# Scattering each slot's expert rows one slot later, and a reordered hand-over into the expert loop, in a GNN and mixture-of-experts kernel

## The chip, the cores and the metric

The kernel runs on one core of one Trainium2 chip. The metric is the device time of one execution in microseconds (us); lower is better. It is written at instruction level: each engine has its own program, and engines wait for one another by semaphores.

## The reference, cut to what matters

```python
# x 2048x512, adj 2048x2048
x = x + gnn(layernorm(x), adj)        # quantised: adj @ relu_q(x_q @ w_q), rounded to 4 bits
h = layernorm(x)
logits = h @ Wr + br                  # 16 experts
topk_w, topk_idx = top_k(softmax(logits), 2); topk_w /= sum(topk_w)
# per token and chosen expert e (hidden size 512):
t = gelu(layernorm(h @ W1[e] + b1[e]) * g1[e] + be1[e])
y = y + topk_w[e] * (t @ W2[e] + b2[e])
x = x + y
```

## The kernel before, in words

The first 200 us or so are the GNN: TensorE (PE) multiplies the adjacency, 128 rows at a time, with the rounded support. The result of each 128-row tile is stored to `out`, its normed copy to `xn_rows` in HBM, and the router's logits give each token two experts. Ranks and hit matrices are made into a table that lays the 4096 (token, expert) pairs out by expert in **slots** of 128 rows. One more piece of the first expert (the "early" slot, names with `e_`) is worked on before the table is complete. `dense` holds the gate values, which SP stores next to the normed rows in `xn_rows`; `tok_i` and `scat_i` are the token indices by slot, `plan` and `begins` packed words that say which expert each slot has and where an expert starts. `words_ps` is the product from which the plan is made, and `table_ok` says that it is there.

Then comes the expert loop, 38 slots, a pair in each trip, on four engines:

- **GpSimd (POOL)**, for slot number s, in this order: `slot_rstd(s + 1)`, the power that gives 1/sigma of the layer norm; `fetch(s)`, which waits for `gate_ok` of slot s + 3 and gathers the rows of slot s + 5 from `xn_rows` by an indirect DMA; `give`, which adds the finished rows of an earlier slot to `out` by an indirect DMA that accumulates. Scatters of neighbouring slots may overlap unless an expert starts between them, since one token is in two experts: `give` waits on `scattered` for that.
- **ScalarE (ACT)**: `slot_gelu(s)`, then `gated(s - 1)`, which turns the second layer's result in PSUM into gated rows `y_sb`, then `slot_x_hi(s + 3)` and `slot_gate(s + 3)` (the latter counts up `gate_ok`), then the rounding of the next expert's weights if one starts.
- **VectorE (DVE)**: `h_hat`, the low halves of the split operands and the statistics.
- **PE**: for slot s, `hidden_t(s)`, `layer_2(s - 1)`, `rows_t(s + 3)`, `layer_1(s + 2)`.

`y_sb` has two buffers, by the slot's parity. Every engine runs its own instructions in order. The lines below are not touched by the diff; they are what ties `gated` on ACT to the scatters on POOL (for slot s = 2j + par, so that `gated(n)` waits until the scatter of slot n - 2 has landed; each of the two semaphores starts at 16 from a store ahead of the loop):

```python
def gated(n, par, landed):
    act.wait_ge(mm2, n + 1)
    act.wait_ge(scattered[par], landed)
    act.activation(y_sb[:, par, :], y_ps(par), ACT.Copy, scale=gate[:, bass.ds(n + 1, 1)]).then_inc(y_ok, 1)
...
    gated(s - 1, 1 - par, landed)
    if not last:
        slot_x_hi(s + 3, 1 - par)
        slot_gate(s + 3, 1 - par, expert_in(word, par + 3))
...
    slot(j * 2 + par, par, word, j * 16 + 16 * par)
```

Of the kernel before, what the change touches and what calls it, by code (L numbers as in the profile page):

```python
# [27 lines left out]
I32 = mybir.dt.int32  # L28
AX_X = mybir.AxisListType.X

P = 128
N = 2048
D = 512
E = 16
T = N // P
C = D // P
# [149 lines left out]
def gnn_moe_program(nc, x, adj_steps, gnn_w, scalars, wr, br, w1, b1, g1, be1, w2, b2, consts, xn_rows, bias_dram, out):  # L186
    with ExitStack() as ctx:
# [5 lines left out]
        def place(name, shape, dt):  # L193
            size = int(np.prod(shape[1:])) * 4
            t = nc.alloc_sbuf_tensor_at(name, shape, dt, offset=where[0])
            where[0] += (size + 31) // 32 * 32
            assert where[0] <= usable, (name, where[0], usable)
            return t

        def sem(name):  # L200
            return ctx.enter_context(nc.semaphore(name))
# [4 lines left out]
        g1_sb = place("g1_sb", [P, E * C], F32)  # L206
        be1_sb = place("be1_sb", [P, E * C], F32)
# [15 lines left out]
        scat_i = place("scat_i", [P, TAB], I32)  # L223
# [55 lines left out]

        e_xg = place("e_xg", [P, ROW], F32)  # L280
        e_h_hat = e_xg[:, 0:D]
        e_y = e_xg[:, 0:D]
        e_gate = place("e_gate", [P, 1], F32)
        e_small = place("e_small", [P, 16], F32)
        e_tok = place("e_tok", [P, 4], I32)
        where[0] = end_gnn - D * 4
        e_g = place("e_g", [P, D], F32)
        where[0] = xg_at
        xg = place("xg", [P, 2, ROW], F32)
        xg1 = place("xg1", [P, ROW], F32)  # L290
# [11 lines left out]
        gt_hi = place("gt_hi", [P, 2, D], F32R)  # L302
        gt_lo = place("gt_lo", [P, 2, D], F32R)
        y_sb = place("y_sb", [P, 2, D], F32)
        idx_s = place("idx_s", [P, 3], I32)
        h_stats = place("h_stats", [P, 2, 6], F32)
        h_mv = place("h_mv", [P, 2, 2], F32)
        h_rs = place("h_rs", [P, 2, 4], F32)
# [26 lines left out]
        def const(name):  # L335
            a, b = COLS[name]
            return k_sb[:, a:b]
# [5 lines left out]
        small_in = sem("small_in")  # L343
# [44 lines left out]
        picked = sem("picked")  # L388
# [23 lines left out]
        idx_ok = sem("idx_ok")  # L412
# [72 lines left out]
        def load_begins(eng, j):  # L485
            return eng.value_load(begins[0:1, bass.ds(j, 1)], min_val=0, max_val=3)

        def expert_in(word, i):

            return (word >> (FIELD * i)) & (E - 1)  # L490
# [116 lines left out]
        @block.gpsimd  # L607
        def _(pool):
            own = Chain(pool, pool_own)
            for h in range(2):  # L610
                half = slice(h * E * C // 2, (h + 1) * E * C // 2)
                pool.dma_start(g1_sb[:, half], g1[:, half]).then_inc(small_in, 16)
                pool.dma_start(be1_sb[:, half], be1[:, half]).then_inc(small_in, 16)
            pool.dma_start(br_sb[:, :], br).then_inc(small_in, 16)
            pool.dma_start(wr_sb[:, :], wr).then_inc(small_in, 16)
            neg_half = const("neg_half")
# [47 lines left out]
            def dense_gates(b):  # L664

                t0, n = GATED[b]
                tiles = slice(t0, t0 + n)
                first, second = (gates[:, 2 + k, tiles].unsqueeze(2).to_broadcast([P, n, E]) for k in range(2))
                if b < 3:
                    pool.wait_ge(gate_parts, b + 1)  # L670
                pool.tensor_tensor(scratch[:, tiles, :], mask[:, 1, tiles, :], second, ALU.mult)
                own.link(pool.tensor_tensor(dense[:, tiles, :], mask[:, 0, tiles, :], first, ALU.mult))
                pool.tensor_tensor(dense[:, tiles, :], dense[:, tiles, :], scratch[:, tiles, :], ALU.add).then_inc(dense_ok, 1)

            def last_gates():

                t0, n = GATED[3]
                tiles = slice(t0, t0 + n)
                pool.wait_ge(picked, 5)
                pool.wait_ge(exp_ok, 5)  # L680
                own.link(pool.tensor_scalar(gates[:, 2, tiles], gates[:, 1, tiles], 1.0, None, ALU.add))
                own.link(pool.tensor_tensor(gates[:, 2, tiles], gates[:, 2, tiles], const("minus_one").to_broadcast([P, n]), ALU.pow))
                own.link(pool.tensor_tensor(gates[:, 3, tiles], gates[:, 1, tiles], gates[:, 2, tiles], ALU.mult))

            def row_hits(b, first, last):

                pool.wait_ge(placed_ok, b + 1)
                if not b:
                    pool.wait_ge(split_lo[0], 1)
                if b in (1, 2):  # L690
                    pool.wait_ge(table_mm, b)
                if b >= 3:
                    pool.wait_ge(adj_mm, STEPS + WINDOWS + 1)
                for j in range(first, last):
                    ins = pool.tensor_scalar(hit_sets[HIT_SET[b]][1][:, j, :], const("minus_row"),
                                             where_f[:, b % 2, 0, j % 2, j // 2:j // 2 + 1], None, ALU.is_equal)
                if last == (2 if b == 4 else 2 * BATCHES[b][1]):
                    ins.then_inc(rows_hit, 1)
# [36 lines left out]
            early_rstd()  # L735
            row_hits(3, 4, 6)
            last_gates()
            row_hits(4, 0, 2)
            dense_gates(3)

            def gather(s):
                to, landed = (xg1[:, :], first_in) if s == 1 else (xg[:, s % 2, :], gathered)
# [8 lines left out]
            def slot_rstd(s, par):  # L751

                pool.wait_ge(h_var, s + 1)
                pool.tensor_tensor(h_rs[:, par, 0:1], h_rs[:, par, 2:3], neg_half, ALU.pow).then_inc(h_rstd, 1)
# [6 lines left out]
            rest = pool.value_load(pairs[0:1, 0:1], min_val=E // 2 - 2, max_val=SLOTS // 2 - 2)  # L761
# [6 lines left out]
            def add_rows(at, par):  # L768
                pool.sem_inc(pool_turn, 1)
                pool.indirect_dma_start(  # L770
                    out, bass.IndirectOffsetOnAxis(ap=at, axis=0),
                    y_sb[:, par, :], None, compute_op=ALU.add).then_inc(scattered[par], 16)

            def give(s, start):

                pool.wait_ge(scattered[s % 2], s // 2 * 16 + 16)
                pool.wait_ge(scattered[1 - s % 2], start * 16 + (s + 1) // 2 * 16)
                pool.wait_ge(y_ok, s + 3)
                add_rows(scat_i[:, s:s + 1], s % 2)
# [6 lines left out]
            slot_rstd(2, 0)  # L786
            fetch(1)
            pool.wait_ge(e_scattered, 16)
            give(0, 1)
            def pool_pair(j):  # L790
                earlier, word = load_begins(pool, j - 1), load_begins(pool, j)
                for s in (2 * j, 2 * j + 1):
                    slot_rstd(s + 1, (s + 1) % 2)
                    fetch(s)
                    give(s - 1, (word & 1) if s % 2 else (earlier >> 1))

            for j in range(1, SURE + 1):
                pool_pair(j)
# [6 lines left out]
            def give_last(back, done, starts):  # L805

                par = (3 - back) % 2
                pool.wait_ge(scattered[par], done)
                pool.wait_ge(scattered[1 - par], starts)
                pool.wait_ge(y_ok, rest * 2 + (4 + back))  # L810
                add_rows(idx_s[:, back:back + 1], par)

            pool.tensor_copy(idx_s[:, :], scat_i[:, bass.ds(rest * 2 + 1, 3)]).then_inc(idx_ok, 1)
            earlier, word = load_begins(pool, rest), load_begins(pool, rest + 1)
            slot_rstd(rest * 2 + 3, 1)
            pool.wait_ge(idx_ok, 1)
            give_last(0, rest * 16 + 16, (earlier >> 1) * 16 + rest * 16 + 16)
            give_last(1, rest * 16 + 32, (word & 1) * 16 + rest * 16 + 16)
            give_last(2, rest * 16 + 32, (word >> 1) * 16 + rest * 16 + 32)
# [7 lines left out]
        def _(act):  # L827
# [143 lines left out]
            store_xn(T - 2)  # L971
            gate_exp(3)
            finish_t(T - 2)
            act.wait_ge(small_in, 96)
            act.wait_ge(last_xn_ok, 1)
            store_xn(T - 1)
            finish_t(T - 1)
# [28 lines left out]
            word = load_plan(act, 0)  # L1006
            rest = act.value_load(pairs[0:1, 0:1], min_val=E // 2 - 2, max_val=SLOTS // 2 - 2)
# [46 lines left out]
            word = load_plan(act, rest + 1)  # L1054
# [457 lines left out]
        def _(pe):  # L1512
# [230 lines left out]
            def first_layer_1_end():  # L1743

                pe.wait_ge(x_lo_ok, 1)
                first_part(xt_lo, 0, last=True).then_inc(mm1, 1)

            pe.wait_ge(tables_in, 16)
            pe.wait_ge(rounded, 1)
            pe.wait_ge(small_in, 96)  # L1750
            for hs in range(2 * WINDOWS):
                half_step(hs)
                for t in range(T - 2):
# [34 lines left out]
            for h in range(2):  # L1788
                ins = pe.matmul(compact_ps, tab_sb[:, h, :], sel[:, h, :].bitcast(F32), start=h == 0, stop=h == 1)
            ins.then_inc(compact_mm, 1)  # L1790
            for kind in range(3):
                for h in range(2):
                    col = 2 * kind + h
                    ins = pe.matmul(words_ps[:, kind * TAB:(kind + 1) * TAB], word_r[:, col:col + 1].to_broadcast([P, P]),
                                    sel[:, h, :], start=h == 0, stop=h == 1)
            ins.then_inc(words_mm, 1)
            first_layer_1_end()
            early_layer_2_lo()
            early_layer_2_end()

# [40 lines left out]
            word = load_plan(pe, 0)  # L1841
            rest = pe.value_load(pairs[0:1, 0:1], min_val=E // 2 - 2, max_val=SLOTS // 2 - 2)
# [24 lines left out]
            before, word = expert_in(load_plan(pe, rest), 1), load_plan(pe, rest + 1)  # L1867
# [57 lines left out]
```

## Time and profile before

| | |
|---|---|
| median of 3 runs | 503.92 us (502.75 to 504.37) |
| the profiled execution | 503.04 us, its span 501.3 us |
| mean granted TensorE clock | 0.984 |
| busy in the span | PE 461.6 us (92%), DVE 348.6 (70%), ACT 285.7 (57%), POOL 233.8 (47%) |
| instructions | 10204 |

The span is what the profiler recorded, 1.7 us less than the execution's own time. In the rows further down, a timeline row is start, duration, engine, source line, operation, output<-inputs; what stands in brackets is how long the engine had been idle before it, and who released it. An indirect DMA's row is the time in which POOL makes its descriptors, and not the transfer, which goes on after it.

### The profile page before, as it was taken

The page shows a single profiled execution, that of the slowest core. Times are in us where ns is not written, and L with a number is a line of the kernel's source. Part 1 is how long each engine was busy: PE and PEld are TensorE (multiplying, and loading weights), DVE is VectorE, ACT ScalarE, POOL GpSimd, SP SyncE. Part 2 cuts the span into 40 slices and gives each one's busy share as a digit, 9 for nine tenths or more (in the row PEclk, how much of TensorE's full clock was granted, in tenths as well). Part 3 has the DMA queues.
Part 4 walks back from the last instruction along what each step waited for, and adds up shares of the span by engine and source line. Part 5 has one row for each costly group of instructions (what it writes and reads, how often), then busy time and mean ns, then how long its engine had stood idle before and what let it go on. Part 6 is the DMA issues. An engine that isn't in the chain of part 4 may idle for free. (4 is left out here: it accounts for less than half of the span.)

```text
span 501.3 us, 10204 instructions
## 1 busy us (share of the span) xinstructions
PE 461.6 (92%) x2297; PEld 379.3 (76%) x2298; DVE 348.6 (70%) x735; ACT 285.7 (57%) x472; POOL 233.8 (47%) x271
## 2 busy tenths in 40 slices
PE   0789999999999999989989999999999999999970
PEld 0568888887888888867868888887888778888850
DVE  5898873868778867875487677486878767786410
ACT  1667453564443442545747857668778865776440
POOL 5364320431174635742464546554455444556531
PEclk9999999999999999989999999999999999999995
DMA  8621224984546362349676876956888888464433
GB/s 288 273 84 43 85 74 165 329 304 149 189 150 228 132 194 103 127 110 310 202 160 162 248 211 140 229 148 165 248 256 230 253 285 195 96 149 73 83 50 42
DMA packets 31451, 87.26 MB, mean 174 GB/s; under 512 B 6016, under 2 KB 6224, under 8 KB 30912
## 3 DMA queue, kind: packets, MB, share of 16 engines
q1 hardware_dynamic: 17488, 56.54, 34.2%
q0 software_dynamic: 9328, 22.02, 21.4%
q10 hardware_dynamic: 4608, 8.39, 4.5%
q8 instruction: 11, 0.18, 0.1%
q14 instruction: 16, 0.13, 0.1%
HBM read 67.79 MB, written 19.14 MB: 173 GB/s over the span
## 5 line engine op out<-in xcount | busy, mean ns | idle before, releaser
L743 POOL DMA_INDIRECT xg<-xn_rows,tok_i x40 | 48.7, 1218 | 86.7 <-ACT gate L967 76.9
L1015 ACT ACTIVATE g_sb<-ps,be_sb,g_sb 128x128 f32<-128x128 f32 x152 | 57.2, 457 | 49.0 <-PE ps L1829 49.0
L770 POOL DMA_INDIRECT out<-y_sb,scat_i x35 | 61.4, 1755 | 28.4 <-DMA out<-y_sb,scat_i 14.6
L1442 DVE TENSOR_TENSOR w_split<-w_raw,w_split x56 | 66.0, 1221 | 9.9 <-issue 9.7
L1450 DVE TENSOR_SCALAR h_hat<-ps,h_mv,h_rs 128x512 f32<-128x512 f32 x38 | 30.7, 809 | 47.1 <-issue 28.4
L833 ACT ACTIVATE adj_hi<-adj_raw,small 128x1024 fp32r<-128x1024 f32 x32 | 36.8, 1150 | 40.6 <-PE ps L1564 34.6
L1001 ACT ACTIVATE w_split<-w_raw x28 | 53.0, 1914 | 4.5 <-DMA w_raw<-in_w 2.6
L1132 DVE SCALAR_TENSOR_TENSOR adj_lo<-adj_raw,small,adj_hi 128x1024 fp32r<-128x1024 f32 x32 | 40.8, 1275 | 19.7 <-ACT adj_hi L833 19.6
L1564 PE MATMUL ps<-sup,adj_lo 128*128 128x512 f32 x192 | 49.2, 398 | 0.0
L1564 PE MATMUL ps<-sup,adj_hi 128*128 128x512 f32 x192 | 49.2, 398 | 0.0
L654 POOL TENSOR_SCALAR rstd<-mv 128x1 f32<-128x1 f32 x15 | 13.7, 915 | 66.7 <-DVE mv L1172 66.7
L1807 PE MATMUL ps<-w_split,gt_hi 128*128 x152 | 41.3, 393 | 0.0
L1810 PE MATMUL ps<-w_split,gt_lo 128*128 x152 | 41.1, 392 | 0.0
L1813 PE MATMUL ps<-w_split,gt_hi 128*128 x152 | 40.8, 390 | 0.0
L994 ACT ACTIVATE y_sb<-ps,gate 128x512 f32<-128x512 f32 x38 | 26.1, 686 | 25.6 <-PE ps L1813 23.8
L1564 PEld LDWEIGHTS ps<-sup,adj_lo 128*128 128x128 f32 x192 | 34.9, 188 | 6.9
L1564 PEld LDWEIGHTS ps<-sup,adj_hi 128*128 128x128 f32 x192 | 35.0, 188 | 6.8
L1807 PE MATMUL ps<-w_split,xt_hi 128*128 x148 | 40.0, 392 | 0.0
L1810 PE MATMUL ps<-w_split,xt_lo 128*128 x148 | 39.8, 390 | 0.0
L1813 PE MATMUL ps<-w_split,xt_hi 128*128 x148 | 39.7, 390 | 0.0
L1668 PE MATMUL ps<-bias_row,two_rows 128*128 (+1 forms) x78 | 37.2, 477 | 0.3 <-DVE x_sb L1166 0.3
L1375 DVE BATCH_NORM_STATS2 h_stats<-ps 128x6 f32<-128x512 f32 x38 | 26.3, 693 | 12.3 <-PE ps L1813 7.5
(212 smaller groups left out, 954.8 us busy)
## 6 DMA issues: line engine op xcount, KB each, us to landing
w_raw<-in_w SPq DMA_DIRECT2D x64, 512.0 KB
adj_raw<-in_adj_steps SPq DMA_DIRECT2D x32, 512.0 KB, 3.5
out<-x_sb ACTq DMA_DIRECT2D x16, 256.0 KB, 2.9
xn_rows<-xn ACTq DMA_DIRECT2D x16, 256.0 KB, 2.7
x_sb<-in_x SPq DMA_DIRECT2D x3, 1024.0 KB, 12.7
gw_raw<-in_gnn_w SPq DMA_DIRECT2D x1, 1024.0 KB, 5.0
x_sb<-in_x SPq DMA_DIRECT2D x2, 512.0 KB, 6.6
xg<-xn_rows,tok_i POOLq DMA_INDIRECT x40, 3.4
```

Of the source, the lines that this page charges most:

```text
L743: return pool.indirect_dma_start(to, None, xn_rows, bass.IndirectOffsetOnAxis(ap=tok_i[:, s:s + 1], axis=0)).then_inc(landed[s % 2], 16)
L770: pool.indirect_dma_start(out, bass.IndirectOffsetOnAxis(ap=at, axis=0), y_sb[:, par, :], None, compute_op=ALU.add).then_inc(scattered[par ...
L833: act.activation(adj_hi[:, par, :], adj_raw[:, par, :], ACT.Copy, scale=small[:, 0:1]).then_inc(adj_hi_ok, 1)
L1001: act.activation(w_parts(n, 0, e + 1), w_raw[:, n, :, :].rearrange("p a n -> p (a n)")[:, at], ACT.Copy).then_inc(split_hi[n], 1)
L1015: ins = act.activation(g_sb[:, par, c * P:(c + 1) * P], ht_ps(par)[:, c * P:(c + 1) * P], ACT.Gelu, scale=g1_sb[:, bass.ds(e * C + c, 1)], ...
L1132: dve.scalar_tensor_tensor(adj_lo[:, par, :], adj_raw[:, par, :], small[:, 0:1], adj_hi[:, par, :].bitcast(F32), ALU.mult, ALU.subtract).t ...
L1442: ins = dve.tensor_tensor(w_parts(n, 1, e + 1, 2 * h, 2), w_raw[:, n, :, :].rearrange("p a n -> p (a n)")[:, at], w_parts(n, 0, e + 1, 2 * ...
L1564: ins = pe.matmul(acc_bank(t), part[:, n % 2, k * P:(k + 1) * P], sup[:, first_k + k, :], start=first_k + k == 0 and not half, stop=first_ ...
L1668: pe.matmul(dst, two_rows[:, :], bias_row[n][:, row], start=True, stop=False)
L1807: pe.matmul(dst, act_hi[:, par, c * P:(c + 1) * P], w_part(n, 0, e, c), start=False, stop=False)
L1810: pe.matmul(dst, act_lo[:, par, c * P:(c + 1) * P], w_part(n, 0, e, c), start=False, stop=False)
L1813: ins = pe.matmul(dst, act_hi[:, par, c * P:(c + 1) * P], w_part(n, 1, e, c), start=False, stop=c == C - 1)
```

## The change

- In the expert loop POOL scatters the rows of slot s - 2 where it scattered those of slot s - 1. The scatter ahead of the loop is gone, and four are behind it instead of three (`give_last(-1, ...)` is new, `idx_s` has four columns). `y_sb`, its two buffers and the wait in `gated` stay.
- Ahead of the loop, PE does the last four products of slot 0's first layer (`first_layer_1_end`) before the six small ones from which the plan is made.
- `last_gates` on POOL no longer waits for `picked`; that wait stands in front of `dense_gates(3)`, which now comes ahead of `row_hits(4, 0, 2)`.
- `g1` and `be1` are loaded by one DMA each, not two, so that POOL issues two fewer at the start.
- The early slot's result `e_y` has the place of `e_g` and not of `e_xg`.

```diff
@@ -279,12 +279,12 @@
         e_h_hat = e_xg[:, 0:D]
-        e_y = e_xg[:, 0:D]
...
         e_g = place("e_g", [P, D], F32)
+        e_y = e_g[:, :]
@@ -302,7 +302,7 @@
-        idx_s = place("idx_s", [P, 3], I32)
+        idx_s = place("idx_s", [P, 4], I32)
@@ -607,10 +607,8 @@
-            for h in range(2):
-                half = slice(h * E * C // 2, (h + 1) * E * C // 2)
-                pool.dma_start(g1_sb[:, half], g1[:, half]).then_inc(small_in, 16)
-                pool.dma_start(be1_sb[:, half], be1[:, half]).then_inc(small_in, 16)
+            pool.dma_start(g1_sb[:, :], g1).then_inc(small_in, 16)
+            pool.dma_start(be1_sb[:, :], be1).then_inc(small_in, 16)
@@ -676,7 +674,6 @@
                 tiles = slice(t0, t0 + n)
-                pool.wait_ge(picked, 5)
                 pool.wait_ge(exp_ok, 5)
@@ -735,8 +732,9 @@
             last_gates()
+            pool.wait_ge(picked, 5)
+            dense_gates(3)
             row_hits(4, 0, 2)
-            dense_gates(3)
@@ -786,13 +784,12 @@
             pool.wait_ge(e_scattered, 16)
-            give(0, 1)
             def pool_pair(j):
-                earlier, word = load_begins(pool, j - 1), load_begins(pool, j)
+                earlier = load_begins(pool, j - 1)
                 for s in (2 * j, 2 * j + 1):
                     slot_rstd(s + 1, (s + 1) % 2)
                     fetch(s)
-                    give(s - 1, (word & 1) if s % 2 else (earlier >> 1))
+                    give(s - 2, 1 if s == 2 else (earlier >> 1) if s % 2 else (earlier & 1))
@@ -808,12 +805,13 @@
-                add_rows(idx_s[:, back:back + 1], par)
-
-            pool.tensor_copy(idx_s[:, :], scat_i[:, bass.ds(rest * 2 + 1, 3)]).then_inc(idx_ok, 1)
+                add_rows(idx_s[:, back + 1:back + 2], par)
+
+            pool.tensor_copy(idx_s[:, :], scat_i[:, bass.ds(rest * 2, 4)]).then_inc(idx_ok, 1)
...
+            give_last(-1, rest * 16 + 16, (earlier & 1) * 16 + rest * 16)
             give_last(0, rest * 16 + 16, (earlier >> 1) * 16 + rest * 16 + 16)
@@ -1788,13 +1786,13 @@
             ins.then_inc(compact_mm, 1)
+            first_layer_1_end()
             for kind in range(3):
...
             ins.then_inc(words_mm, 1)
-            first_layer_1_end()
             early_layer_2_lo()
```

How the change moves instructions, at three places. First POOL where the loop is entered, before the change: `h_rs` is `slot_rstd`, `xg<-xn_rows` a gather, `out<-y_sb` a scatter, and a row of L777 is the ordering wait in `give`.

```order
L754 TENSOR_TENSOR h_rs<-h_rs,k_sb 128x1 [waits h_var]
L743 DMA xg<-xn_rows,tok_i 128x528 [waits gate_ok]
L770 DMA out<-y_sb,scat_i 2176x512 [waits y_ok,scattered1,e_scattered,scattered0]
L486 TENSOR_LOAD begins
L486 ISA x2
L486 TENSOR_LOAD begins
L486 ISA x2
L754 TENSOR_TENSOR h_rs<-h_rs,k_sb 128x1 [waits h_var]
L743 DMA xg<-xn_rows,tok_i 128x528 [waits gate_ok]
L777 ISA [waits scattered1]
L770 DMA out<-y_sb,scat_i 2176x512 [waits scattered0,y_ok]
```

The same place with the change (lines stand two lower):

```order
L752 TENSOR_TENSOR h_rs<-h_rs,k_sb 128x1 [waits h_var]
L741 DMA xg<-xn_rows,tok_i 128x528 [waits gate_ok]
L486 TENSOR_LOAD begins [waits e_scattered]
L486 ISA x2
L752 TENSOR_TENSOR h_rs<-h_rs,k_sb 128x1 [waits h_var]
L741 DMA xg<-xn_rows,tok_i 128x528 [waits gate_ok]
L768 DMA out<-y_sb,scat_i 2176x512 [waits y_ok,scattered0,scattered1]
L752 TENSOR_TENSOR h_rs<-h_rs,k_sb 128x1 [waits h_var]
L741 DMA xg<-xn_rows,tok_i 128x528 [waits gate_ok]
```

The first scatter, that of slot 0, moved behind the next `h_rs` and the next gather, and each later one with it.

Second, POOL ahead of the loop, before the change: `gates` is `last_gates`, `scratch` and `dense` are `dense_gates(3)`, and `hit_row_139` is `row_hits(4, 0, 2)`.

```order
L681 TENSOR_SCALAR gates<-gates 128x5 [waits exp_ok,picked]
L682 TENSOR_TENSOR gates<-gates,k_sb 128x5 [waits pool_own]
L683 TENSOR_TENSOR gates<-gates 128x5 [waits pool_own]
L695 TENSOR_SCALAR hit_row_139<-k_sb,where_f 128x128 [waits adj_mm,placed_ok,pool_own]
L695 TENSOR_SCALAR hit_row_139<-k_sb,where_f 128x128
L671 TENSOR_TENSOR scratch<-mask,gates 128x80
L672 TENSOR_TENSOR dense<-mask,gates 128x80
L673 TENSOR_TENSOR dense<-dense,scratch 128x80 [waits pool_own]
```

And with the change:

```order
L678 TENSOR_SCALAR gates<-gates 128x5 [waits exp_ok]
L679 TENSOR_TENSOR gates<-gates,k_sb 128x5 [waits pool_own]
L680 TENSOR_TENSOR gates<-gates 128x5 [waits pool_own]
L669 TENSOR_TENSOR scratch<-mask,gates 128x80 [waits picked,pool_own]
L670 TENSOR_TENSOR dense<-mask,gates 128x80
L671 TENSOR_TENSOR dense<-dense,scratch 128x80 [waits pool_own]
L692 TENSOR_SCALAR hit_row_139<-k_sb,where_f 128x128 [waits adj_mm,placed_ok]
L692 TENSOR_SCALAR hit_row_139<-k_sb,where_f 128x128
```

The wait for `picked` went from the first row to the fourth, and the three `dense_gates` rows ahead of the two hit rows.

Third, PE just ahead of the loop, before the change: `sel,tab_sb` is the table product, `sel,word_r` the products for the plan, and `w_split,xt_lo` is `first_layer_1_end`.

```order
L1789 MATMUL ps<-sel,tab_sb 128x54 [waits xn_t_ok,sel_ok,tab_ok]
L1789 MATMUL ps<-sel,tab_sb 128x54
L1794 MATMUL ps<-sel,word_r 128x54 x6
L1727 MATMUL ps<-w_split,xt_lo 128x512 [waits x_lo_ok]
L1727 MATMUL ps<-w_split,xt_lo 128x512 x3
L1673 MATMUL ps<-w_split,bias_hi 128x512 [waits split2_lo]
```

And with the change:

```order
L1787 MATMUL ps<-sel,tab_sb 128x54 [waits xn_t_ok,sel_ok,tab_ok]
L1787 MATMUL ps<-sel,tab_sb 128x54
L1725 MATMUL ps<-w_split,xt_lo 128x512 [waits x_lo_ok]
L1725 MATMUL ps<-w_split,xt_lo 128x512 x3
L1793 MATMUL ps<-sel,word_r 128x54 x6
L1671 MATMUL ps<-w_split,bias_hi 128x512 [waits split2_lo]
```

The four products of slot 0's layer one went ahead of the six for the plan.

## Rows read from the trace of the kernel before

**Rows 1.** The page's first part: busy us, share of the span, instructions.

```profile
PE 461.6 (92%) x2297; PEld 379.3 (76%) x2298; DVE 348.6 (70%) x735; ACT 285.7 (57%) x472; POOL 233.8 (47%) x271
```

**Rows 2.** Stages: length, busy us (instructions) by engine, granted clock, DMA share, GB/s.

```profile
300.00:340.00 40.00, 40.00 (x200) 33.06 (x199) 26.42 (x43) 26.96 (x51) 22.73 (x18) 1.00 0.72 181
...
216.00:218.00 2.00, 2.00 (x6) 1.62 (x5) 0.97 (x2) 0.04 (x1) 1.10 (x1) 0.50 0.00 0
```

**Rows 3.** Timeline late in the loop, ACT and POOL, slots 33 to 35.

```profile
465.29 0.69 ACT L994 ACTIVATE y_sb<-ps,gate 128x512 f32<-128x512 f32 x1 [0.78 <-PE ps L1813]
...
466.84 1.36 POOL L743 DMA_INDIRECT xg<-xn_rows,tok_i  x1 [2.31 <-DMA out<-y_sb,scat_i]
...
468.51 1.61 POOL L770 DMA_INDIRECT out<-y_sb,scat_i  x1 [0.30 <-issue]
...
472.12 0.69 ACT L994 ACTIVATE y_sb<-ps,gate 128x512 f32<-128x512 f32 x1 [0.74 <-PE ps L1813]
...
475.00 1.59 POOL L770 DMA_INDIRECT out<-y_sb,scat_i  x1 [0.30 <-issue]
...
479.26 0.69 ACT L994 ACTIVATE y_sb<-ps,gate 128x512 f32<-128x512 f32 x1 [1.11 <-PE ps L1813]
```

**Rows 4.** Timeline where the loop is entered, ACT, POOL and PE.

```profile
239.49 1.64 POOL L770 DMA_INDIRECT out<-y_sb,scat_i  x1 [0.30 <-issue]
...
241.54 0.69 ACT L994 ACTIVATE y_sb<-ps,gate 128x512 f32<-128x512 f32 x1 [0.88 <-PE ps L1813]
...
248.67 0.69 ACT L994 ACTIVATE y_sb<-ps,gate 128x512 f32<-128x512 f32 x1 [1.04 <-DMA out<-y_sb,scat_i]
...
252.51 0.66 PE L1829 MATMUL ps<-k_sb,h_hat 128*128 128x128 f32 x4 [0.96 <-DVE h_hat L1450]
...
260.91 0.66 PE L1829 MATMUL ps<-k_sb,h_hat 128*128 128x128 f32 x4 [1.27 <-DVE h_hat L1450]
```

**Rows 5.** Timeline of POOL, two neighbouring scatters, the second waiting.

```profile
400.35 2.04 POOL L770 DMA_INDIRECT out<-y_sb,scat_i  x1 [1.53 <-DMA out<-y_sb,scat_i]
...
410.44 1.58 POOL L770 DMA_INDIRECT out<-y_sb,scat_i  x1 [4.79 <-DMA out<-y_sb,scat_i]
```

**Rows 6.** DMA busy tenths, 466 to 494 us in 40 slices of 0.7 us.

```profile
DMA  6000559795000365978000009881000058996860
```

**Rows 7.** Timeline of POOL behind the loop, the scatters of slots 35 and 36.

```profile
480.80 1.62 POOL L770 DMA_INDIRECT out<-y_sb,idx_s  x1 [3.47 <-ACT y_sb L994]
486.87 1.56 POOL L770 DMA_INDIRECT out<-y_sb,idx_s  x1 [4.44 <-issue]
```

**Rows 8.** DMA queues, 241 to 441 us: packets, MB, share of 16 engines.

```profile
q1 hardware_dynamic: 7017, 25.30, 39.0%
```

**Rows 9.** Timeline ahead of the loop, POOL, PE and DVE.

```profile
208.99 0.34 POOL L681 TENSOR_SCALAR gates<-gates 128x5 f32<-128x5 f32 x1 [1.76 <-DVE so_far L1226]
...
214.15 0.68 DVE L1371 TENSOR_TENSOR xt_lo<-ps,xt_hi 128x512 fp32r<-128x512 f32 x1
...
214.78 0.83 PE L1794 MATMUL ps<-sel,word_r 128*128 128x54 f32 x6
...
215.44 2.03 PE L1727 MATMUL ps<-w_split,xt_lo 128*128 128x512 f32 x4
...
216.41 1.10 POOL L743 DMA_INDIRECT xg<-xn_rows,tok_i  x1 [2.77 <-DMA xn_rows<-dense]
...
217.51 0.70 DVE L1375 BATCH_NORM_STATS2 h_stats<-ps 128x6 f32<-128x512 f32 x1 [1.03 <-PE ps L1727]
...
218.64 0.32 DVE L1424 TENSOR_SCALAR fields<-ps 128x162 f32<-128x162 f32 x1
...
219.86 0.42 PEld L1721 LDWEIGHTS ps<-k_sb,xg 128*128 128x128 f32 x4 [0.26 <-DMA xg<-xn_rows,tok_i]
```

**Rows 10.** Timeline of the first microseconds, POOL.

```profile
3.22 0.53 POOL L613 DMA_DIRECT2D be_sb<-in_be  x1
...
10.31 0.60 POOL L626 TENSOR_TENSOR x_pow<-x_pow,k_sb 128x1 f32<-128x1 f32 x1 [3.66 <-DVE x_pow L1094]
```

More of the change, by code:

```diff
@@ L973, in _ @@
             finish_t(T - 2)
-            act.wait_ge(small_in, 96)
+            act.wait_ge(small_in, 64)
             act.wait_ge(last_xn_ok, 1)
@@ L1749, in _ @@
             pe.wait_ge(rounded, 1)
-            pe.wait_ge(small_in, 96)
+            pe.wait_ge(small_in, 64)
             for hs in range(2 * WINDOWS):
```

## The prediction, made before the changed kernel ran

> **What bounds the kernel now.** I read the page's first part first: PE is busy for 92% of the span and POOL for 47% [rows 1]. The table of stages then says where PE is the limit: 40.00 of 40 us between 300 and 340, with 200 matmuls, at the full granted clock [rows 2]. So in the expert loop nobody holds PE up, except at its entry, where two gaps stand in its timeline (0.96 and 1.27 us, both for `h_hat`) [rows 4]. One slot takes 6.83 us there (from one `y_sb` write to the next) [rows 3], and over the loop 6.99 us: `y_sb` of slot 1 is written at 241.54 [rows 4], that of slot 35 at 479.26 [rows 3], 34 slots in 237.72 us.
>
> Next I read who waits for a scatter, since that is what moves. The wait of ACT on `scattered` bites once before the change: `y_sb` of slot 2 at 248.67, released by the DMA of slot 0's scatter, which POOL had issued at 239.49 [rows 4]. In all other slots the scatter lies so far back that the wait is met, and that distance is what the change uses up.
>
> **The scatter one slot later: the term that decides.** `gated(n)` on ACT may write its buffer only when the scatter of slot n - 2 has landed, and this stays. The late rows give the distances. ACT writes `y_sb` at 465.29, and when it has copied the gate, POOL gathers at 466.84 and scatters at 468.51; the next `y_sb` is written at 472.12 [rows 3]. The scatter at 468.51 is that of the slot just written, and the write that needs its buffer is the next but one, at 479.26: the distance is 479.26 - 468.51 = 10.75 us. With the change, the scatter at this place is that of the slot before, whose buffer is wanted at 472.12, so 472.12 - 468.51 = 3.61 us are left.
>
> How long does a scatter take? From the start of its row to the end of its transfer, where the DMA engines are otherwise quiet: the one issued at 480.80 [rows 7] has its data moving from slice 24 to slice 27 of the DMA row, so until about 485.6 [rows 6], 4.8 us; that of 468.51 [rows 3] ends in slice 9, by 473.0 [rows 6], 4.5 us at most. POOL's next ordered scatter started 6.07 us after 480.80 [rows 7], so a released engine starts some time after the data. With ACT I put 0.6 us on top of 4.6: 5.2 us in the quiet case (an estimate; its lower end is 4.5 with nothing on top). Where weights are loaded too, it is longer: 248.67 - 239.49 = 9.18 us on ACT [rows 4], 410.44 - 400.35 = 10.09 us on POOL [rows 5]. All of it is above 3.61 us.
>
> So ACT will stand still in every slot, and that is a ring, since ACT's own instructions release the scatter: `gated(n - 1)` → gate copy → `gate_ok` → POOL's gather → scatter of n - 2 → it lands → `gated(n)`. Its length is the new time of a slot. The first half is 468.51 - 465.29 = 3.22 us, or 475.00 - 472.12 = 2.88 [rows 3]; I take 3.1. The second half is the scatter's: 5.2 in quiet, some 8.0 beside loads (the two rows less 1 to 2 us, since they are ones long enough to be seen waiting). The loads' queue held 39% of the DMA engines' time from 241 to 441 us, with the other queue beside it [rows 8]. The same bytes spread over a longer loop meet fewer of the scatters, so I take 45% of slots as loaded: 0.45 x 8.0 + 0.55 x 5.2 = 6.5 us. The ring is then 3.1 + 6.5 = 9.6 us, against 6.99 now. From `gated(1)`, the last that needs no scatter, to `gated(35)` that is 34 x (9.6 - 6.99) = **+88.7 us**. The bounds: all quiet, 34 x (2.88 + 5.2 - 6.99) = +37 us; all loaded, 34 x (3.22 + 8.0 - 6.99) = +144 us. Nothing is hidden below the lower one, unless a scatter comes back in under 3.9 us (6.99 - 3.1), which no row shows.
>
> A rule of the skill speaks on just this number. The Trainium skill (DMA: Bandwidth & Descriptors, section on the anatomy of one DMA on the SWDGE path) fits a DMA from GpSimd as 2.0 us plus its bytes at 436 GB/s, 2.6 us for the 256 KB here; by it the ring would be 5.7 us and hold nobody. The DMA row disagrees: 4.5 to 4.8 us in the quietest stretch.
>
> What else stands in the ring's shadow: PE will wait 9.6 - 6.83 = 2.8 us in a slot, for `xt_hi` that ACT writes behind `gated`. DVE's split of it and the statistics come later with it. POOL's `slot_rstd` runs once in each round, behind the scatter, and PE uses its result a slot later.
>
> **The four behind the loop.** In place of three; the scatter of slot 34 needs nothing but its turn. Those of 35, 36 and 37 follow their `y_sb` as before, and `gated(36)` and `gated(37)` follow the landings of 34 and 35: 480.80 is 1.54 us behind 479.26, and 486.87 is 7.61 behind it [rows 3, 7], distances that already hold one landing. One more scatter on the queue: 0 to 2 us, I take 0.5.
>
> **The hand-over.** The layer's four products (2.03 us, in a stretch where the granted clock is 0.50 [rows 2]) go ahead of the six small ones (0.83 us) [rows 9]. PE begins the six at 214.78, and `xt_lo`, for which the four wait, is there at 214.15 + 0.68 = 214.83, so that they can begin at about 214.9 and end at 217.0 instead of 217.47; the statistics start at about 217.0 instead of 217.51 [rows 9], the power and `h_hat` with them, and the plan's DVE work behind them too: -0.5 us. The six small ones end at about 217.8, before DVE wants them at 218.1, half a microsecond ahead of the 218.64 of before [rows 9]. The gates: without `picked` POOL's row at 208.99, idle for 1.76 us before it, can begin at about 207.6 [rows 9], and `dense` is done some 2.8 us sooner; the gather at 216.41 waited for that store, and will next wait for `tok_i`, which DVE makes from the table product; I take it as 1.0 us sooner. PE had idled 0.26 us for it [rows 9], so it adds at most that. I take -0.5 us for the whole, bounds 0 and -1. If the cover of the small products is gone (DVE waiting for the plan), it costs their 0.83 us.
>
> **Things at nothing.** Two DMA issues fewer at the start save 2 x 0.53 us of POOL, which then idles 3.66 us for DVE anyhow [rows 10]. The place of `e_y` and the fourth index column change no work. The two gaps of 0.96 and 1.27 us at the entry [rows 4] would go, since POOL no longer stands in front of a scatter there; but the ring is longer than the slot with its gap, so this gives nothing more: they are in the 6.99.
>
> **Sum.** 88.7 + 0.5 - 0.5 = +88.7 us on the profiled 503.04, which lies 0.9 below the median of the three runs: 503.9 + 88.7 = 592.6; I say 591, as both estimated shares lean high.
>
> **The rivals.**
> - *No ring, and faster* (3%). If scatters came back within 3.61 us (the point from which it decides), ACT would never wait, and POOL would do the next slot's `slot_rstd` without standing behind a landing. Then the two gaps go: 503.9 - 0.96 - 1.27 - 0.5 = 501.2. For it: only the page's 2.6 us. Against it: every landing that a row shows. No change, within 0.3% (502.4 to 505.4): 2%.
> - *A ring in loaded slots only* (4%). If the quiet landing fits into the slot after all, say because the gather goes out sooner against the scatter, only some 15 slots pay about 2 us: +30, or 534.
> - *PE's clock becomes the bound* (4%). PE now pauses in each slot. The granted clock did fall to 0.50, at 216 to 218, after a stretch of small products and waits [rows 2, 9]. If it stayed at that level (1.2 GHz for 2.4) through the loop, a slot would be twice 6.83, 13.7 us: 34 x 6.7 = +227, or 731. Against it: layer two of slot n needs only what `gated(n - 2)` released, and after it has two rounds (19.2 us) for one and a half slots of work; at half speed PE would also be busy without a pause. The Trainium skill (TensorE: Matmul & The Clock Gate, Part 1) has the clock halved after idling and doubled after sustained work, by which it would toggle and hide under the ring.
>
> **How the numbers follow.** The ring in every slot has 87%, at 591, between 541 and 647. The range 552 to 628 leaves 7% of that at its ends and the 13% of the others outside, so it holds 80%. Faster by over 0.3% (what a measurement of this kernel can tell) 3%, within it 2%, slower 95%.
>
> **What would show it.** In the profile of the changed kernel: `y_sb` on ACT idle in nearly every slot, released by the DMA of `out<-y_sb`, 3 to 4 us each; a scatter 3.1 us behind each `y_sb`; the loop's `y_sb` rows 8.1 to 11 us apart, farther while weights are loaded and nearest 8.1 at the end; PE's share down from 92% to about 78%; `h_stats` of slot 0 half a microsecond sooner. It is wrong if the `y_sb` rows stay near 6.9 us apart, or if the wait in a slot is for PE.

## The result: 13.7% slower, 572.02 us

| | before | with the change |
|---|---|---|
| median | 503.34 us (502.59 to 504.37, 4 runs) | 572.02 us (570.62 to 574.83, 4 runs) |
| ratio | | 1.1372, 95% interval 1.1344 to 1.1401 |
| span of the profiled run | 501.3 us | 573.1 us |
| mean granted TensorE clock | 0.984 | 0.971 |

The forecast was 591, with a range of 552 to 628. The cause that it named is in the profile; the size was 19 us too large. The profiled execution of the changed kernel took 574.83 us, 2.8 above the median, so its rows add up to a little more than the medians differ.

The page of the changed kernel first: busy time, share of the span and instructions by engine, then three of its costliest groups, with the idle time in front of them and who ended it.

```profile
PE 478.5 (84%) x2297; PEld 383.9 (67%) x2298; DVE 350.9 (61%) x735; ACT 284.3 (50%) x472; POOL 227.0 (40%) x269
...
L741 POOL DMA_INDIRECT xg<-xn_rows,tok_i x40 | 44.6, 1116 | 192.6 <-ACT gate L965 188.4
L992 ACT ACTIVATE y_sb<-ps,gate 128x512 f32<-128x512 f32 x38 | 26.2, 688 | 135.3 <-DMA out<-y_sb,scat_i 131.6
L1440 DVE TENSOR_TENSOR w_split<-w_raw,w_split x56 | 66.1, 1221 | 10.5 <-ACT w_split L999 7.3
```

PE's work is the same 2297 matmuls, but 84% and not 92% of the span [rows 1]. `y_sb` on ACT, which sat idle for a scatter's DMA once before (1.04 us) [rows 4], does so for 131.6 us. The list of waits says how often (engine and line that waited, for whom, us in all, times, longest):

```profile
POOL xg L741 <- ACT gate L965: 188.4, 37, 8.9
ACT y_sb L992 <- DMA out<-y_sb,scat_i: 131.6, 34, 8.9
DVE xt_lo L1369 <- ACT xt_hi L960: 72.7, 27, 6.5
...
PE ps L1827 <- DVE h_hat L1448: 37.1, 24, 2.6
```

34 times, which is every slot but the first two, which need no scatter, and the two written behind the loop, which wait for the scatters of `idx_s`. The table of stages has the 40 us that stood in [rows 2]: PE did 153 matmuls in it, not 200, and was busy for 33.31 us and not 40.00. The DMA engines had less to do, too (0.62 for 0.72).

```profile
300.00:340.00 40.00, 33.31 (x153) 26.04 (x152) 21.51 (x35) 22.03 (x43) 16.22 (x15) 0.96 0.62 165
```

The ring itself, late in the loop where no weights are loaded; first ACT and then POOL in the changed kernel's timeline (start, duration, engine, line, operation; in brackets the idle time and its releaser):

```profile
527.43 0.69 ACT L992 ACTIVATE y_sb<-ps,gate 128x512 f32<-128x512 f32 x1 [2.54 <-DMA out<-y_sb,scat_i]
...
528.50 0.20 ACT L965 ACTIVATE gate<-xg  x1
...
535.21 0.69 ACT L992 ACTIVATE y_sb<-ps,gate 128x512 f32<-128x512 f32 x1 [3.30 <-DMA out<-y_sb,scat_i]
...
543.10 0.69 ACT L992 ACTIVATE y_sb<-ps,gate 128x512 f32<-128x512 f32 x1 [4.38 <-DMA out<-y_sb,scat_i]
...
528.99 1.02 POOL L741 DMA_INDIRECT xg<-xn_rows,tok_i  x1 [4.34 <-ACT gate L965]
530.31 1.56 POOL L768 DMA_INDIRECT out<-y_sb,scat_i  x1 [0.30 <-issue]
531.37 1.12 POOL L752 TENSOR_TENSOR h_rs<-h_rs,k_sb 128x1 f32<-128x1 f32 x1
536.76 1.02 POOL L741 DMA_INDIRECT xg<-xn_rows,tok_i  x1 [4.27 <-ACT gate L965]
538.09 1.59 POOL L768 DMA_INDIRECT out<-y_sb,scat_i  x1 [0.31 <-issue]
```

Read it as a circle: `y_sb` at 527.43, gate copy, gather at 528.99, scatter at 530.31 (2.88 us behind `y_sb`), and the next `y_sb` at 535.21, 4.90 us behind the scatter. 2.88 + 4.90 = 7.78 us, and the slot takes just that. The same circle with a weight load beside it:

```profile
377.88 0.69 ACT L992 ACTIVATE y_sb<-ps,gate 128x512 f32<-128x512 f32 x1 [0.85 <-DMA out<-y_sb,scat_i]
378.95 0.20 ACT L965 ACTIVATE gate<-xg  x1
379.44 1.73 POOL L741 DMA_INDIRECT xg<-xn_rows,tok_i  x1 [3.91 <-ACT gate L965]
...
380.88 0.82 SPq L532 DMA_DIRECT2D w_raw<-in_w  x2
381.47 1.57 POOL L768 DMA_INDIRECT out<-y_sb,scat_i  x1 [0.30 <-issue]
...
382.75 0.87 SPq L532 DMA_DIRECT2D w_raw<-in_w  x2
390.09 0.69 ACT L992 ACTIVATE y_sb<-ps,gate 128x512 f32<-128x512 f32 x1 [7.08 <-DMA out<-y_sb,scat_i]
```

SP issues the loads of two layers around the scatter, each in two halves; the scatter comes back after 8.62 us, and the slot takes 12.21 us. POOL's gather took 1.73 us here and not 1.02, so the first half of the circle was longer too (3.59 us). Over the whole loop, `y_sb` of slot 1 is written at 244.60 and that of slot 35 at 551.31:

```profile
244.60 0.69 ACT L992 ACTIVATE y_sb<-ps,gate 128x512 f32<-128x512 f32 x1 [0.89 <-PE ps L1811]
...
551.31 0.69 ACT L992 ACTIVATE y_sb<-ps,gate 128x512 f32<-128x512 f32 x1 [2.75 <-DMA out<-y_sb,scat_i]
```

306.71 us for 34 slots, 9.02 us each, against 6.99. By the distances between the `y_sb` rows, 11 of these slots took 9.4 to 12.6 us (11.36 on average, their scatters back after 8.3 us), and 23 took 7.6 to 8.5 (7.90 on average, their scatters back after 5.0). In each of the 11, SP issued a weight load between 1.5 us before and 0.9 us after the start of the scatter's row. Of the 23, one had a load issued while its scatter was out, 3.6 us behind the row's start. The span grew by 71.8 us: 69.0 in these 34 slots, 3.1 ahead of them (slot 1 at 244.60 and not 241.54; see the first experiment), and -0.3 behind them.

### The profile page after: what moved, and what is told of

The parts are those of the page before. It is cut to its first block and busy times, and to the rows that moved or that the text cites. A ratio compares the mean times of both kernels' runs of the same rounds, so it can differ in the third digit from the quotient of the medians.

```text
span 573.1 us, 10152 instructions
## 1 busy us (share of the span) xinstructions
PE 478.5 (84%) x2297; PEld 383.9 (67%) x2298; DVE 350.9 (61%) x735; ACT 284.3 (50%) x472; POOL 227.0 (40%) x269
## 5 line engine op out<-in xcount | busy, mean ns | idle before, releaser
L741 POOL DMA_INDIRECT xg<-xn_rows,tok_i x40 | 44.6, 1116 | 192.6 <-ACT gate L965 188.4
L992 ACT ACTIVATE y_sb<-ps,gate 128x512 f32<-128x512 f32 x38 | 26.2, 688 | 135.3 <-DMA out<-y_sb,scat_i 131.6
L1369 DVE TENSOR_TENSOR xt_lo<-ps,xt_hi 128x512 fp32r<-128x512 f32 x39 | 26.9, 690 | 72.7 <-ACT xt_hi L960 72.7
L768 POOL DMA_INDIRECT out<-y_sb,scat_i x34 | 53.8, 1581 | 10.4 <-issue 10.4
L1827 PE MATMUL ps<-k_sb,h_hat 128*128 128x128 f32 x152 | 24.6, 285 | 39.5 <-DVE h_hat L1448 37.1
L1130 DVE SCALAR_TENSOR_TENSOR adj_lo<-adj_raw,small,adj_hi 128x1024 fp32r<-128x1024 f32 x32 | 40.8, 1276 | 19.7 <-ACT adj_hi L831 19.6
L1827 PEld LDWEIGHTS ps<-k_sb,h_hat 128*128 128x128 f32 x152 | 16.7, 141 | 52.7 <-DVE h_hat L1448 48.5
L1805 PE MATMUL ps<-w_split,xt_hi 128*128 x148 | 42.5, 411 | 9.4 <-ACT xt_hi L960 9.4
L752 POOL TENSOR_TENSOR h_rs<-h_rs,k_sb 128x1 f32<-128x1 f32 x38 | 44.1, 1160 | 4.4 <-DVE h_rs L1376 4.3
L1808 PE MATMUL ps<-w_split,gt_lo 128*128 x152 | 43.8, 413 | 0.0
L1805 PE MATMUL ps<-w_split,gt_hi 128*128 x152 | 43.7, 411 | 0.0
L1811 PE MATMUL ps<-w_split,gt_hi 128*128 x152 | 42.3, 401 | 0.3 <-DVE w_split L1440 0.2
L1811 PE MATMUL ps<-w_split,xt_hi 128*128 x148 | 39.8, 390 | 0.5 <-DVE w_split L1440 0.5
```

The lines of the kernel that those rows point to most:

```text
L741: return pool.indirect_dma_start(to, None, xn_rows, bass.IndirectOffsetOnAxis(ap=tok_i[:, s:s + 1], axis=0)).then_inc(landed[s % 2], 16)
L768: pool.indirect_dma_start(out, bass.IndirectOffsetOnAxis(ap=at, axis=0), y_sb[:, par, :], None, compute_op=ALU.add).then_inc(scattered[par ...
L1130: dve.scalar_tensor_tensor(adj_lo[:, par, :], adj_raw[:, par, :], small[:, 0:1], adj_hi[:, par, :].bitcast(F32), ALU.mult, ALU.subtract).t ...
L1805: pe.matmul(dst, act_hi[:, par, c * P:(c + 1) * P], w_part(n, 0, e, c), start=False, stop=False)
L1808: pe.matmul(dst, act_lo[:, par, c * P:(c + 1) * P], w_part(n, 0, e, c), start=False, stop=False)
L1811: ins = pe.matmul(dst, act_hi[:, par, c * P:(c + 1) * P], w_part(n, 1, e, c), start=False, stop=c == C - 1)
```

## The experiments

Nine runs were made, one kernel among them twice, on three occasions, each beside the kernel before on the same chip; the ratio is what counts. Two theories: the **ring** (`gated` waits for the scatter of two slots back, and that scatter now follows the `y_sb` just ahead), and its rivals (POOL's new order or a late scatter costs by itself; the hand-over has a part in it).

| kernel | median us | before there | ratio, 95% interval |
|---|---|---|---|
| hand_over_only | 502.72 | 502.20 | 1.0005 (0.9982 to 1.0028) |
| scatter_only | 571.76 | 502.20 | 1.1356 (1.1297 to 1.1415) |
| scatter_before_gate | 500.15 | 502.20 | 0.9963 (0.9938 to 0.9987) |
| scatter_then_gather | 553.01 | 502.20 | 1.1018 (1.0965 to 1.1071) |
| four_buffers | 505.94 | 503.02 | 1.0056 (1.0032 to 1.0079) |
| thin_loads | 535.73 | 503.02 | 1.0645 (1.0611 to 1.0679) |
| scatter_before_gate_2 | 501.79 | 503.38 | 0.9971 (0.9951 to 0.9992) |
| before_gate_no_hand_over | 502.37 | 503.38 | 0.9989 (0.9974 to 1.0004) |
| before_gate_four_buffers | 499.97 | 503.38 | 0.9946 (0.9920 to 0.9971) |

### The two halves of the change

`hand_over_only` is the kernel before with the diff's parts on `g1`/`be1`, `e_y`, `last_gates`, `dense_gates(3)` and `first_layer_1_end`; `scatter_only` has the other parts (`idx_s`, `give(s - 2, ...)`, `give_last(-1, ...)`).

> The kernel before with all of the change except the scatter: sooner gates, slot 0's layer one ahead of the words, two DMA issues fewer, e_y on e_g. The statistics of slot 0 started 1.03 us sooner in the changed kernel, so my sum now allows 0 to -1.0 us, middle -0.5: 502.9. Rival: a part of the 69 us comes from the hand-over, since slot 1's y_sb was written at 244.60 there and at 241.54 before; by it this kernel is slower by up to 3 us, 506.

> The kernel before with the later scatter alone. If the ring through ACT's wait for the landed scatter is the whole cause, 571 to 573, within 1.5 us of the changed kernel. If the hand-over costs 3 us of its own, 569 or less.

The scatter alone is 571.76, as the ring theory expected: all of the loss. The hand-over alone makes no difference that this measurement can tell. The rows of `hand_over_only` that answer to [rows 9], and the table product just ahead of them (`sel,tab_sb`):

```profile
214.28 0.62 PE L1787 MATMUL ps<-sel,tab_sb 128*128 128x54 f32 x4 [0.56 <-ACT tab_sb L985]
...
216.34 0.69 DVE L1373 BATCH_NORM_STATS2 h_stats<-ps 128x6 f32<-128x512 f32 x1
...
219.84 0.66 PE L1719 MATMUL ps<-k_sb,xg 128*128 128x128 f32 x4 [1.29 <-DMA xg<-xn_rows,tok_i]
...
221.37 1.11 PE L1827 MATMUL ps<-k_sb,h_hat 128*128 128x128 f32 x4 [0.88 <-issue]
235.52 0.66 PE L1719 MATMUL ps<-k_sb,xg 128*128 128x128 f32 x4 [1.77 <-DMA xg<-xn_rows,tok_i]
```

The statistics start at 216.34 (217.51 before), yet PE's next product with gathered rows is where it was (219.84, with 1.29 us of idle time for the gather in front of it). Most of that 1.17 us is not the new order's doing. The kernel before had the table product at this time:

```profile
214.34 0.62 PE L1789 MATMUL ps<-sel,tab_sb 128*128 128x54 f32 x4 [0.52 <-ACT tab_sb L987]
```

Counted from the table product, all eleven traces compare:

| traces | granted clock where the four products ran | statistics behind the table product | gathered product behind it |
|---|---|---|---|
| before | 0.50 | 3.17 us | 5.54 us |
| two others with the old order (`scatter_only`, `before_gate_no_hand_over`) | 1.00 | 2.32 us | 5.50 and 5.63 us |
| the eight with the new order | 1.00 | 2.06 to 2.07 us | 5.41 to 5.56 us |

So at the same clock the new order brings the statistics 0.25 us sooner, and PE's next product, which waits for the gather, not at all. A further 0.85 us is the clock, which was low there in the trace of before and in no other.

The 3.1 us at the loop's entry are not shown to be the hand-over's either. Slot 1's `y_sb` stood between 240.5 and 244.6 us in the kernels with the hand-over; without it, it stood at 244.07 in `scatter_only` and at 241.33 in `before_gate_no_hand_over`. What goes with a late entry is the clock. In four traces it fell to 0.50 for 2 to 4 us around 224 (0.91 on average from 220 to 240), and there slot 1's `y_sb` came 28.4 to 30.2 us behind the table product. In the other seven it stayed at 1.00 from 220 to 240, and that distance was 26.1 to 27.2 us. `scatter_only`, with the old order, is one of the four. PE had waited alike ahead of it in both kinds (1.2 to 1.5 us for the gather, then 0.9), so what decides is open. PE's wait for a later gather, near 235 us, differs too: 3.06 us in the changed kernel, the longest, 1.77 in `hand_over_only` and 1.45 in `scatter_only`.

### Cutting the ring at POOL

```diff
                 for s in (2 * j, 2 * j + 1):
                     slot_rstd(s + 1, (s + 1) % 2)
-                    fetch(s)
                     give(s - 2, 1 if s == 2 else (earlier >> 1) if s % 2 else (earlier & 1))
+                    fetch(s)
```

> The changed kernel with the scatter of slot s-2 behind slot_rstd(s+1) as changed, but ahead of the wait for the gate instead of behind the gather. That cuts one edge of the ring: the scatter no longer follows the y_sb before it. Ring theory: 6.9 us a slot again, 501 to 504 us in all, with the two gaps at the loop's entry (0.96 and 1.27 us) gone. Rival (a scatter that is late by one slot costs by itself, by its order behind the power or by its meeting the loads): 540 or more.

500.15 us, a little under the expected 501 to 504, and 6.99 us a slot in its profile: the ring no longer sets the time, with the same scatter (slot s - 2), the same `slot_rstd` ahead of it and the same four behind the loop. What decided was that the scatter stood behind the wait for a gate which ACT copies after the `y_sb` before. ACT still waited for a scatter 11 times, 29.2 us in all and up to 5.0 at a time, but those waits hardly reached PE, which waited 3.7 us from 236 to 490 us (3.9 before).

### Cutting it at ACT

`y_sb` gets seven buffers where the adjacency was: four used in turn in the loop, three for the last slots. The wait in `gated` is for one scatter of the same parity less.

```diff
+                to = y_sb[:, at, :] if at is not None else y_sb[:, n & 3, :] if isinstance(n, int) else \
+                    y_sb[:, :, :].rearrange("p a d -> p (a d)")[:, bass.ds((n & 3) * D, D)]
-                act.wait_ge(scattered[par], landed)
+                if at is None and not (isinstance(landed, int) and landed <= 16):
+                    act.wait_ge(scattered[par], landed - 16)
...
-            with act.Fori(1, SURE + 1) as j:
+            act_pair(1)
+            with act.Fori(2, SURE + 1) as j:
...
-                    y_sb[:, par, :], None, compute_op=ALU.add).then_inc(scattered[par], 16)
+                    y_sb[:, slot, :], None, compute_op=ALU.add).then_inc(scattered[par], 16)
```

> The changed kernel with its POOL order untouched, but four y_sb buffers in the loop instead of two (three more for the slots behind it), so that ACT waits for the scatter of slot n-4 and not n-2. That cuts the ring at its other edge. Ring theory: 6.9 us a slot, 501 to 504 us. Rival (POOL's order, or contention of late scatters, and not the buffer): 560 or more.

505.94 us, with POOL's order untouched. So neither the order nor the lateness costs 69 us; the buffer's wait does. It is 2 us above the range that I had expected, and 0.56% above the kernel before: the four buffers with this order leave a cost of their own. POOL's list of waits from 236 to 490 us (line, for whom, us in all, times, longest) is where one looks:

```profile
POOL xg L743 <- ACT gate L972: 52.4, 28, 3.4
POOL out L770 <- DMA out<-y_sb,scat_i: 27.6, 9, 4.6
POOL h_rs L754 <- DVE h_rs L1387: 16.8, 15, 3.9
```

POOL stands before a scatter for the landing of another 9 times, 27.6 us in all; in the kernel before it was 6 times and 14.6 us over the same stretch. These are the ordering waits where an expert starts, with the next slot's power and gather queued behind them. That this is the 3 us is not shown: over the same stretch PE's own waits add up to 4.9 us, against 3.9 in the kernel before. `before_gate_four_buffers`, below, has the same buffers and is faster than before, so the buffers by themselves don't cost it.

### Making the ring shorter

```diff
                     slot_rstd(s + 1, (s + 1) % 2)
-                    fetch(s)
+                    pool.wait_ge(gate_ok, s + 4)
                     give(s - 2, 1 if s == 2 else (earlier >> 1) if s % 2 else (earlier & 1))
+                    gather(s + 5)
```

> The changed kernel with scatter and gather exchanged behind the wait for the gate: the ring is shorter by the gather's 1.02 us and the 0.30 us behind it, 1.33 us. Quiet slots go from 7.84 to the 6.85 that PE needs (22 of them, -22 us), loaded ones from some 11.3 to 10.0 (12, -16 us): 534 us, between 526 and 540. If something else than this ring sets the slot's time, the exchange changes little: 565 or more.

553.01 us, so 19 us gone and not 38; the expectation was missed. The way it was worked out is what failed, as the timeline shows (ACT's `y_sb` and gate, then POOL):

```profile
505.11 0.69 ACT L993 ACTIVATE y_sb<-ps,gate 128x512 f32<-128x512 f32 x1 [1.76 <-DMA out<-y_sb,scat_i]
506.17 0.20 ACT L966 ACTIVATE gate<-xg  x1
512.53 0.69 ACT L993 ACTIVATE y_sb<-ps,gate 128x512 f32<-128x512 f32 x1 [2.95 <-DMA out<-y_sb,scat_i]
...
507.37 1.69 POOL L768 DMA_INDIRECT out<-y_sb,scat_i  x1 [3.51 <-ACT gate L966]
509.36 1.00 POOL L741 DMA_INDIRECT xg<-xn_rows,tok_i  x1 [0.30 <-issue]
```

The scatter starts 2.26 us behind `y_sb`, not at the 1.56 where the gather had started: 1.00 us lies between the end of the gate copy (506.37) and the scatter, against 0.29 (528.70 to 528.99) for the gather in the changed kernel. Nearly every slot has the same two numbers. The exchange thus takes 2.88 - 2.26 = 0.62 us out of the ring and not 1.33, and 34 x 0.62 = 21 us is what went (the loop's slots took 8.42 us each, 0.60 less). That the 0.7 us are the scatter's own waits and register work, which before had passed while the gather ran, is the likely reading; it wasn't tried alone. The exchange settles one more thing: with the gather behind the scatter, scatters were back after 5.0 us on average in 23 slots and after 8.5 in 11, much as in the changed kernel, so it is not the gather in front of them that makes them long.

### Thinner weight loads

From expert 4's second layer on, each half of a layer is loaded by 32 of its 1024 columns.

```diff
+            def load_thin(n, h, at, par):
+                sp.dma_start(w_raw[:, n, par, h * HALF:h * HALF + 32],
+                             w_dram[n][at, h * HALF:h * HALF + 32]).then_inc(raw_in[n], 16)
...
+            sp_pair(1, False)
+            with sp.Fori(2, E // 2 - 1) as j:
+                sp_pair(j, True)
```

> The changed kernel, but from expert 4's second layer on each weight load fetches 32 of 1024 columns of its half, so that the rest of the loop computes with old weights: its output is not the reference's, the number of instructions and waits stays. If the loaded slots (12 of 34, 9.4 to 12.6 us) owe their length to the weight loads beside the scatter, about 9 of them fall to 7.84 us: 9 x (11.3 - 7.84) = 31 us, so 541, between 534 and 546. If the long landings have another cause (the gather in front on the same queue), 565 or more.

535.73 us, within the expected range. Four slots in the middle of its loop (`y_sb` rows of ACT):

```profile
322.00 0.69 ACT L1000 ACTIVATE y_sb<-ps,gate 128x512 f32<-128x512 f32 x1 [2.54 <-DMA out<-y_sb,scat_i]
329.68 0.69 ACT L1000 ACTIVATE y_sb<-ps,gate 128x512 f32<-128x512 f32 x1 [4.21 <-DMA out<-y_sb,scat_i]
337.47 0.69 ACT L1000 ACTIVATE y_sb<-ps,gate 128x512 f32<-128x512 f32 x1 [2.53 <-DMA out<-y_sb,scat_i]
345.16 0.69 ACT L1000 ACTIVATE y_sb<-ps,gate 128x512 f32<-128x512 f32 x1 [2.35 <-DMA out<-y_sb,scat_i]
```

7.68 to 7.79 us each, and 7.90 over the 34; no slot took more than 8.8. So the long slots are long because of the weight loads, and the ring without them still costs 535.73 - 503.02 = 33 us. Of the 69 us, about half is the ring and half the loads that lengthen it.

### A slightly faster version

> The kernel scatter_before_gate once more, on another occasion, beside the kernel before: 0.9963 (0.9938 to 0.9987) was measured. If it is a real gain of 1 to 3 us, the ratio is again under 0.999; if it was chance, 1.000.

> The kernel before with the later scatter, placed behind slot_rstd and ahead of the wait for the gate, and nothing else of the change. If the gain of scatter_before_gate is POOL's power no longer standing behind a scatter's wait (gaps of 0.96 and 1.27 us at the entry), it is here too: 501 to 502 where before is 503. If it was the hand-over, this one equals before.

> scatter_before_gate with the four y_sb buffers. ACT still waited for scatters there, up to 5 us in a slot with weight loads. If these waits reach PE, the buffers give another 1 to 2 us, 499 to 501; if PE does not see them, it equals scatter_before_gate; if the buffers themselves cost the 3 us by which four_buffers lay above before, about 503.

`scatter_before_gate` came out ahead of before a second time (0.9971). Without the hand-over it is 0.9989, an interval that holds 1 and overlaps the others, so what share the hand-over has in it stays open. With the four buffers it is 0.9946, some 2.7 us faster than before; it has the lowest ratio, but its interval overlaps that of `scatter_before_gate`, so that the buffers add to the gain is not shown. PE's waits in its loop, from 236 to 490 us, are down to two groups:

```profile
PE ps L1838 <- issue: 0.8, 1, 0.8
PE ps L1838 <- DVE h_hat L1459: 0.8, 2, 0.5
```

Before, over the same stretch, PE waited 3.5 us for `h_hat` and 0.4 for nothing that the profile shows. Two of these waits are the gaps at the loop's entry [rows 4], with POOL's power standing behind a scatter, and no trace with the later scatter has them. So with the four buffers PE waits 2.3 us less, and the 34 slots took 235.0 us in this profile, 2.7 less than before. In `scatter_before_gate` other waits for `h_hat` come later in the loop: its two profiles have 3.7 and 2.5 us in all (the first is of an execution of 503.07 us, well above its median), and `before_gate_no_hand_over` has 2.4. That the lost gaps are what makes these kernels faster fits these rows, and no run shows it by itself.

## Why the prediction was right, and what was mis-sized

- **What bounds the loop; the ring.** Right, in place and kind. The prediction had 3.61 us left for a scatter and took 5.2 as needed, 4.5 at the least; a quiet scatter was back on ACT after 4.7 to 5.3 us, 5.0 on average. The signs it named came too: ACT's wait in each slot (0.7 to 8.9 us, 3.9 on average), and `y_sb` rows 7.6 to 12.6 us apart, farther where weights are loaded.
- **The size.** 19.7 us too much in the loop: 34 x 9.6 = 326.4 was predicted, 306.7 measured. The first half of the ring is 2.88 us in most slots, 2.96 on average, and not 3.1 (5 us). The share of loaded slots was the term most mis-sized: 45% were taken, 11 of 34 or 32% are (about 12 us). The landings themselves were close: 5.2 for 5.0 in quiet (5 us too much), 8.0 for 8.3 when loaded (3 us too little). The last 1.3 us is the rounding of 9.56 to 9.6. That the time came within 3.3% owes something to luck: the loaded share was a guess.
- **Who holds PE.** Only partly right. I had it wait for `xt_hi`; it did so 7 times for 9.4 us, but 24 times for `h_hat`, 37.1 us: DVE's statistics stand behind `xt_lo`, which waits for `xt_hi` (72.7 us), and POOL's power behind the late scatter. The ring's length is the same, so it changed no number. PE's share came out at 84%, not 78%, since the ring was shorter and some matmuls ran at the lower clock: over the 34 slots PE was busy for 251 us, against 234 before for the same work.
- **The four behind the loop.** 0.5 us taken; the time from `y_sb` of slot 35 to the span's end went from 22.0 to 21.8 us.
- **The hand-over.** -0.5 us was taken, and nothing can be told from its own run. Two steps were off. The 2.03 us of the four products belonged to the low clock of one execution; at the full clock they take 1.20, and the new order brings the statistics 0.25 us sooner and not 0.5. And the gather was taken as 1.0 us sooner, with at most 0.26 us for PE to wait; PE's product with the gathered rows did not move, so PE waits 1.2 to 1.3 us for the gather, and nothing of the gain is left there.
- **The rivals.** No ring: it needed a return within 3.61 us, and 4.7 us was the least. The 2.6 us by the Trainium skill (DMA: Bandwidth & Descriptors, the section on the anatomy of one DMA) are not what an accumulating scatter takes in any of these traces. None landed less than 4.5 us after the start of its row. A ring in loaded slots only: all 34 had it. The clock as the bound: it fell now and then (0.96 between 300 and 340), at times for most of a slot (0.81 from 335.4 to 343.2, with PE busy throughout), but ACT still waited for its scatter in all 34 slots, 0.66 us at the least, so it hid under the ring.

## What to carry to other kernels

- Before an operation that frees a buffer is moved later, write down who waits for the buffer and what that engine must do to release the moved operation. If the second leads back to the first, the loop's period is the length of that circle, whatever the busy shares say; here POOL was busy for 47% and PE for 92%, and a circle through POOL, its DMA and ACT came to set the time.
- Measure the distance that is there (10.75 us) against the transfer's return (4.7 to 9.7 us) and the loop's period (6.9): one step later left 3.61 us.
- A circle can be cut at any edge. Placing the scatter ahead of the wait, rather than behind it, meant moving one line, and the scatter is still one slot later than before.
- Before a gain is put down to a new order, look at the granted clock where it is read, in more than one execution. Of the 1.17 us by which the statistics came sooner here, 0.25 was the order's.

## What the runs showed of the hardware that had not been expected

- An accumulating scatter of 128 rows of 2 KB, issued from GpSimd, was back on the waiting engine 5.0 us on average (4.7 to 5.3) after its row began in the 23 slots without weight loads near its start, and after 8.3 us on average (6.5 to 9.7) in the 11 beside 1 MB weight loads, though the loads were issued from another engine on another queue. Thinning the loads took the long ones away (5.4 us at most).
- Behind the same wait on POOL, a gather started 0.28 to 0.29 us after the gate copy's end in the changed kernel's slots, and a scatter 0.99 to 1.08 us after it in those of `scatter_then_gather` (one of 1.33).
- The same stretch of program had TensorE's granted clock at 0.50 in one execution and at 1.00 in others: where the plan is made, only in the trace of before; around 224 us, in four traces of eleven.
